# Transposing the tail rows of each routed tile on TensorE in place of VectorE

## The reference

```python
x = x + xattn(_layernorm(x), ctx_512, Wq, Wkv_expand, Wout)
x = x + bitlinear_ffn(_layernorm(x), ...)
x = x + moe(_layernorm(x), rms_weight, router_w, w_gate, w_up, w_down, sw_gate, sw_up, sw_down)

# moe, per token t with h = rmsnorm(x):
probs = softmax(h @ router_w); topv, topi = top_k(probs, 2); topv /= sum(topv)
g, u  = einsum('td,edf->tef', h, w_gate), einsum('td,edf->tef', h, w_up)
eo    = einsum('tef,efd->ted', silu(g) * u, w_down)
moe   = einsum('te,ted->td', w_dense, eo)          # 8 experts of 1024 x 512, 2 per token
out   = moe + silu(h @ sw_gate) * (h @ sw_up) @ sw_down
```

## Time and profile before

| | us |
|---|---|
| median of three runs | 651.04 (650.00 to 651.28) |
| profiled execution, its own time | 651.04 |
| its span | 648.9 |

### The profile page before, as it was taken

How to read it: one execution, slowest core, us unless ns; L and a number is a source line. 1 busy time by engine, 2 the same in 40 slices (tenths; PEclk the granted TensorE clock), 3 DMA queues, 4 the chain that set the end, 5 groups by cost and what they waited for, 6 DMA issues and landing times.

```text
span 648.9 us, 10501 instructions
## 1 busy us (share of the span) xinstructions
PE 614.7 (95%) x3604; PEld 477.7 (74%) x3605; DVE 527.8 (81%) x897; ACT 424.2 (65%) x559; POOL 147.7 (23%) x146
## 2 busy tenths in 40 slices
PE   5889999998999999969999997999999999999996
PEld 4678888886887444434557886988989889898875
DVE  5778888888587779989899558697897978979687
ACT  3988888779655969976465355376493663946530
POOL 3263446425000333427900220000000000000041
PEclk9999999999999999989999997999999999999999
DMA  8967776765236998835999556775967859678347
GB/s 329 398 271 300 299 299 234 299 259 194 98 134 253 419 384 319 331 130 201 417 377 381 194 221 232 279 310 211 375 233 277 328 209 361 227 282 342 129 152 277
DMA packets 31068, 177.87 MB, mean 274 GB/s; under 512 B 4064, under 2 KB 4064, under 8 KB 14784
## 3 DMA queue, kind: packets, MB, share of 16 engines
q1 hardware_dynamic: 25536, 158.64, 63.5%
q0 software_dynamic: 5504, 18.88, 7.7%
HBM read 154.30 MB, written 23.20 MB: 274 GB/s over the span
## 4 chain that ended last, share of the span: by engine, by line
PE 39%; DVE 23%; ACT 17%; issue 14%; DMA 3%; DVEq 2%; SPq 1%; ACTq 0%
PE BK L305 9%; PE BK L2025 9%; DVE WL L1005 7%; ACT PR L1364 5%; PE BK L2028 3%; PE BK L1771 3%; PE BK L1872 3%; ACT WH L1549 2%; PE BK L311 2%; ACT RA L1337 2%; PE BK L317 2%; PE BK L312 2%; DMA RA<-wbit 2%; DMA RX<-wqk 2%; DVE BH L887 1%
## 5 line engine op out<-in xcount | busy, mean ns | idle before, releaser
L2025 PE MATMUL BK<-EX,WH 128*128 128x320 f32 x512 | 136.2, 348 | 3.6 <-DVE EX L1030 3.2
L2028 PE MATMUL BK<-EX,WL 128*128 128x160 f32 x448 | 106.8, 238 | 0.0
L2025 PEld LDWEIGHTS BK<-EX,WH 128*128 128x128 f32 x512 | 94.2, 192 | 6.1 <-issue 3.5
L1005 DVE TENSOR_TENSOR WL<-RA,WH 128x2048 fp32r<-128x2048 f32 x40 | 89.3, 2288 | 9.6 <-ACT WH L1549 9.4
L2028 PEld LDWEIGHTS BK<-EX,WL 128*128 128x128 f32 x448 | 87.0, 194 | 0.3
L1549 ACT ACTIVATE WH<-RA 128x2048 fp32r<-128x2048 f32 x40 | 73.7, 1912 | 2.4 <-PE BK L1872 2.3
L682 POOL DMA_INDIRECT GA<-rows,SLOT x4 | 4.9, 1231 | 246.6 <-DVE WL L1005 245.7
L650 POOL TENSOR_TENSOR HB<-HB,ND (+2 forms) x28 | 31.2, 1129 | 104.8 <-DVE BH L887 104.1
L1434 ACT ACTIVATE RA<-RA,RT 128x2048 int16<-128x2048 f32 x22 | 44.2, 2020 | 9.8 <-DMA RA<-wbit 6.6
L1005 DVE TENSOR_TENSOR WL<-RC,WH 128x2048 fp32r<-128x2048 f32 x20 | 45.0, 2287 | 0.6 <-ACT WH L1549 0.6
L1826 PE MATMUL BK<-TG,XQ 128*128 128x512 bf16 x192 | 42.4, 379 | 0.1
(11 more groups left out here) (306 smaller groups left out, 1571.5 us busy)
## 6 DMA issues: line engine op xcount, KB each, us to landing
RA<-wbit SPq DMA_DIRECT2D x54, 1024.0 KB, 6.4
RA<-wmoe SPq DMA_DIRECT2D x40, 1024.0 KB, 6.5
RC<-wmoe SPq DMA_DIRECT2D x20, 1024.0 KB, 7.6
rows<-ZERO POOLq DMA_DIRECT2D x40, 256.0 KB, 12.7
XG<-rows SPq DMA_DIRECT2D x10, 512.0 KB, 3.6
rows<-YS SPq DMA_DIRECT2D x9, 512.0 KB, 6.1
RA<-wqk SPq DMA_DIRECT2D x7, 640.0 KB, 7.8
RA<-wo SPq DMA_DIRECT2D x4, 1024.0 KB, 7.3
```

Source lines behind the costliest of these rows:

```text
L1005: e.tensor_tensor(WL[m][:, q * RAW:q * RAW + RAW], RC[j][:, :], WH[m][:, q * RAW:q * RAW + RAW].bitcast(f32), ALU.subtract)\
L2025: mm = e.matmul(bank[GBK[f]][:, 0:2 * R], WH[m][:, at], EX[:, k, :, :].rearrange("p a b -> p (a b)"), start=k == 0, stop=k == KD - 1)
L2028: e.matmul(bank[GBK[f]][:, 0:R], WL[m][:, at], EX[:, k, 0, :], start=False, stop=False)
```

## The change

The tail rows are no longer transposed on VectorE. TensorE transposes them, 32 rows and 128 columns at a time, each right behind the full block of the same columns and into the same bank, so that a bank holds up to three blocks of 160 columns. That needs three banks per tile (`TB` = 0, 1, 3) in place of two, with three, three and two blocks (`TK`). The buffer `XT` goes. ScalarE and VectorE read whole blocks of 160 columns from the banks, three instructions each. The third group waits for the product that frees bank 3. In the opening of the routed part VectorE's order changes, and the third tail load of SP loses a wait.

```diff
-TB = (0, 1)
-TB_FIRST = (4, 5)
+TK = ((0, 1, 2), (3, 4, 5), (6, 7))
+TB = (0, 1, 3)
+TB_FIRST = (4, 5, 3)
...
             e.wait_ge(s("et_pe"), 2 * NS + 2)
             e.dma_start(XG[:, :], rows_dram[2 * R:2 * R + P, :]).then_inc(s("e_in"), 16)
-            e.wait_ge(s("et_lo"), 3 * NS + 1)
             e.dma_start(XY[XTAIL, :], rows_dram[2 * R + P:3 * R, :]).then_inc(s("e_in"), 16)
...
-            def tail_rows(t):
-                waits(e, ("e_in", t * 32 + 32))
-                for j in range(4):
-                    at = slice(TAIL_R * j, TAIL_R * j + TAIL_R)
-                    ins = e.transpose(XT[at, :, :], r3(XY[XTAIL, :], KD)[:, :, at])
-                ins.then_inc(s("et_lo"), 1)
             def routed_lo(t, at=TB):
-                for q in range(2):
...
+                for n, ks in enumerate(TK):
+                    e.wait_ge(s("et_hi"), t * 3 + n + 1)
+                    ins = e.tensor_tensor(EX[:, ks[0]:ks[-1] + 1, 1, :], r3(bank[at[n]][:, 0:R * len(ks)], len(ks)),
+                                          EX[:, ks[0]:ks[-1] + 1, 0, :].bitcast(f32), ALU.subtract)
+                    if n != 1:
                         ins.then_inc(s("et_lo"), 1)
...
             split(1, 0, (0,))
             e.wait_ge(s("rows"), 1)
+            hidden(NS - 1, HTKH, HTKL)
+            routed_lo(NS, TB_FIRST)
             split(1, 0, (1,))
-            hidden_product(NS - 1)
-            e.wait_ge(s("eh"), 2 * NS)
-            tail_rows(NS)
-            routed_lo(NS, TB_FIRST)
-            hidden_lo(NS - 1, HTKH, HTKL)
             split(1, 1)
...
                 gate_sum(t, 1)
-                tail_rows(t + 1)
                 routed_product(t)
...
             def routed_hi(t, at=TB):
-                for q in range(2):
-                    e.wait_ge(s("et_pe"), t * 2 + q + 1)
-                    e.activation(EX[:, 4 * q:4 * q + 4, 0, 0:P], r3(bank[at[q]], 4), ACT.Copy).then_inc(s("et_hi"), 1)
-                e.wait_ge(s("et_lo"), t * 3 + 1)
-                e.activation(EX[:, :, 0, P:R], XT[:, :, :], ACT.Copy).then_inc(s("et_hi"), 1)
+                for n, ks in enumerate(TK):
+                    if n < 2:
+                        e.wait_ge(s("et_pe"), t * 2 + n + 1)
+                    e.activation(EX[:, ks[0]:ks[-1] + 1, 0, :], r3(bank[at[n]][:, 0:R * len(ks)], len(ks)), ACT.Copy)\
+                        .then_inc(s("et_hi"), 1)
...
-            def routed_rows(t, at=TB):
-                waits(e, ("e_in", t * 32 + 32))
-                for q in range(2):
-                    rows_t(q, XG, at)
+            def routed_rows(t, ns, at=TB):
+                for n in ns:
+                    if n == 0:
+                        waits(e, ("e_in", t * 32 + 32))
+                    for i, k in enumerate(TK[n]):
+                        cs = slice(k * P, k * P + P)
+                        e.transpose(bank[at[n]][:, i * R:i * R + P], XG[:, cs], IDF[:, :])
+                        m = e.transpose(bank[at[n]][:, i * R + P:i * R + R], XY[XTAIL, cs], IDF[XTAIL, XTAIL])
+                    if n != 1:
+                        m.then_inc(s("et_pe"), 1)
...
-                    routed_rows(NS, TB_FIRST)
+                    e.wait_ge(s("ys_d"), NS)
+                    routed_rows(NS, (0, 1, 2), TB_FIRST)
...
                 waits(e, ("hsum", t * 5 + 3))
-                routed_rows(t + 1)
+                routed_rows(t + 1, (0, 1))
+                waits(e, ("hsum", t * 5 + 4))
+                routed_rows(t + 1, (2,))
```

More of the change, by code:

```diff
@@ L219, in program @@
         SI = c("SI", [P, FE], f32)
-        XT = nc.alloc_sbuf_tensor_at("XT", [P, KD, TAIL_R], f32, offset=HTH.manual_sbuf_range[0] + 4 * KE * 2 * R)
         assert c.at == HB.manual_sbuf_range[0]
@@ L1012, in rows_lo @@
                     e.tensor_tensor(EX[:, 4 * q:4 * q + 4, 1, 0:P], r3(bank[4 + q], 4),
-                                    EX[:, 4 * q:4 * q + 4, 0, 0:P].bitcast(f32), ALU.subtract).then_inc(s("et_lo"), 1 + q)
-            def tail_rows(t):
-                waits(e, ("e_in", t * 32 + 32))
-                for j in range(4):
-                    at = slice(TAIL_R * j, TAIL_R * j + TAIL_R)
-                    ins = e.transpose(XT[at, :, :], r3(XY[XTAIL, :], KD)[:, :, at])
-                ins.then_inc(s("et_lo"), 1)
-            def routed_lo(t, at=TB):
-                for q in range(2):
[L1024 to L1027, removed]
+                                    EX[:, 4 * q:4 * q + 4, 0, 0:P].bitcast(f32), ALU.subtract).then_inc(s("et_lo"), 1)
+            def routed_lo(t, at=TB):
+                for n, ks in enumerate(TK):
[3 more added lines that the diff above has]
+                    if n != 1:
                         ins.then_inc(s("et_lo"), 1)
-                e.wait_ge(s("et_hi"), t * 3 + 3)
-                e.tensor_tensor(EX[:, :, 1, P:R], XT[:, :, :], EX[:, :, 0, P:R].bitcast(f32), ALU.subtract)\
-                    .then_inc(s("et_lo"), 1)
             def gate_sum(t, q):
@@ L1606, in result @@
             def result(t):
-                waits(e, ("y2_pe", t + 1), ("y_st", t * 32 + 32), ("et_lo", t * 3 + 3))
+                waits(e, ("y2_pe", t + 1), ("y_st", t * 32 + 32), ("et_lo", t * 2 + 2))
                 e.activation(YS[:, 0:512], bank[AB[0]], ACT.Copy)
@@ L1651, in _ @@
             e.wait_ge(s("ys_d"), NS)
-            e.wait_ge(s("ht_lo"), 2 * NS)
             e.wait_ge(s("cnt"), 1)
@@ L1944, in ranks, with rows_t @@
                 m.then_inc(s("pos_pe"), 1)
-            def rows_t(q, rows, at=(4, 5)):
+            def rows_t(q, rows):
                 for k in range(4):
                     cs = slice((4 * q + k) * P, (4 * q + k + 1) * P)
-                    m = e.transpose(bank[at[q]][:, k * P:k * P + P], rows[:, cs], IDF[:, :])
+                    m = e.transpose(bank[4 + q][:, k * P:k * P + P], rows[:, cs], IDF[:, :])
                 m.then_inc(s("et_pe"), 1)
-            def routed_rows(t, at=TB):
-                waits(e, ("e_in", t * 32 + 32))
-                for q in range(2):
-                    rows_t(q, XG, at)
+            def routed_rows(t, ns, at=TB):
[8 more added lines that the diff above has]
+                        m.then_inc(s("et_pe"), 1)
             def routing(step):
@@ L1974, in tile @@
                 if not more:
-                    waits(e, ("et_lo", t * 3 + 3))
+                    waits(e, ("et_lo", t * 2 + 2))
                 for m in range(2):
@@ L1983, in tile @@
                             routing((m, q))
-                    e.wait_ge(s("et_lo"), t * 3 + 3)
+                    e.wait_ge(s("et_lo"), t * 2 + 2)
                     lows(e, bank[m], [(EX[:, k, 1, 0:P], WH[m][:, k * FE:k * FE + FE]) for k in range(KD)])\
```

## The result

| | before | after |
|---|---|---|
| median, us | 650.95 | 684.38 |
| range of the runs | 650.00 to 651.28 | 683.93 to 686.18 |
| profiled execution, its own time | 651.04 | 685.42 |
| its span | 648.9 | 683.6 |

The changed kernel is slower by 5.2% (ratio 1.0521, 95% interval 1.0499 to 1.0544). The forecast was slower by 0.6%, 654.6 us: the right sign, and a tenth of the size. The measured time lies far outside the forecast's range of 651.8 to 658.6 us.

A forecast was written before the change was run, and what follows sets the result against it. The loop was taken as bound by a 26.83 us chain through TensorE, VectorE and ScalarE, with TensorE 0.29 us from binding. Loop 1.8, end 0.55 and opening 1.2 gave 3.55 on 651.04: 654.6 us, range 651.8 to 658.6.

The forecast's parts named there:

- VectorE's saving is worth nothing in the loop: Routed loop: VectorE's 1.77 us of XT transposes are off the chain, paid back as longer wait; 0 us gain.
- 0.29 us of cover on TensorE: Routed loop: TensorE's gate-sum wait hides 0.29 us per period; the remaining 0.26 us over seven periods gives +1.8 us.
- What is added on TensorE: Each routed tile: eight small transposes at 0.069 us, spacing taken from L1933, 0.55 us per tile.
- each switch costs extra: Rival, routed tiles: each switch between 32 and 128 rows costs extra, 1.28 us per tile; 660.4 us, chance 0.05.
- my high end: TensorE's added work per tile: 1.28 us if each small transpose alternating with a full one cost 0.16 us.
- Opening: Opening of the routed part: TensorE waits for WL0's second half, starts 1.6 us later; less clock saving, +1.2 us.
- the 0.4 us that I took off: Opening: assumed saving from less work run at half clock, 0.4 us between 0.7 or 0.6 and nothing.
- End: Last routed tile: no next gate sum to hide behind, so the whole added 0.55 us counts; +0.55 us.
- the wait on hsum 5t+4: Routed loop: new wait costs nothing, as that product is issued before TensorE finishes its last part and twelve transposes.
- ScalarE's EX copies in the loop: Three copies keep 1280 columns in all, cost 0; the second, waiting for all sixteen transposes, causes no wait.
- SP's wait: Opening: dropping SP's wait on et_lo lets one load leave about 2 us earlier; worth 0.
- Signs set beforehand: Forecast wrong if period stays 26.8 or exceeds 27.4 us, or TensorE starts the first tile no later than before.

The follow-up runs named there:

- experiment 2: Changed kernel with all eight full transposes of a tile first and all eight small ones behind them; 655.83 us, ratio 1.0079 to the kernel before.
- experiment 7: Changed kernel with the opening's old order restored on VectorE (second WL0 half ahead of the EX low parts); 679.41 us, ratio 1.045 to the kernel before.
- experiment 4: Kernel before, with the eight full transposes of each routed tile issued four times over, 32 in a row; 666.67 us, ratio 1.0257.

## Why the prediction was right in sign and wrong in size

- **VectorE's saving is worth nothing in the loop: right.** All 1.77 us of it, and more, came back as its longer wait before L1032 (0.36 to about 3.1).
- **0.29 us of cover on TensorE, the rest lengthens the period: right** as a mechanism. With the small ones last (experiment 2) the period grew by 0.50 us for 0.78 us of added work, so 0.28 was covered.
- **The step that failed: "What is added on TensorE", 0.069 us per small transpose, 0.55 us per tile.** That is the cost within a run of equals, and L1933 was such a run. The changed kernel alternates. Each change of height adds 0.13 us, sixteen a tile are 2.1 us, and with 8 x 0.062 for the small ones themselves the added work is 2.6 us, nearly five times the forecast. My rival "each switch costs extra" named the mechanism and priced it at half, 1.28 us a tile from a single gap of 0.16 us, with a chance of 0.05; even its 660.4 us is 24 too low. An upper bound was in the rows: a lone transpose lasts 0.27 us against a spacing of 0.110, so a change that lets nothing overlap costs up to 0.16 by this estimate. Sixteen of them on top of the 0.55 are 3.1 us a tile, above the 2.6 measured, where my high end was 1.28. The Trainium skill says in TensorEngine Tiling (Array Packing), Key Properties, that changing the tiling mode drains TensorE. If the small transposes run in another mode than the full ones, which no view shows, the traces agree: a cost at every change of height, 0.13 us each.
- **The clock in the loop: not in the forecast at all.** This is the second step that failed, a term put at nothing: I looked for idle stretches only, and there is none. 12.6 of the 33 us, 1.6 us in each of eight tiles, come from half clock behind an unbroken run of full and small transposes in turn. No rival had it.
- **Opening: mechanism right, size short.** TensorE waited for the second half of WL0, as worked out. It started 2.8 us later and not 1.6, because the sixteen transposes ended at 394.1 and not 392.7, and everything behind them moved with that. The half clock lasted 10.2 us and not 6.8, so there was no saving to subtract: the 0.4 us that I took off had the wrong sign, and about 0.3 came on top. 3.1 in place of 1.2.
- **End: mechanism right.** The whole of a tile's added work counts there: 4.2 us, which is 2.6 and 1.6.
- **Edits costed at nothing held**: the wait on hsum 5t+4, ScalarE's EX copies in the loop, SP's wait. ScalarE did come to wait for transposes, which the sum had excluded (L1575, 11.5 us over eight tiles), but off the path: TensorE never waited for it in the loop.
- **Signs set beforehand.** I had called the forecast wrong if the period came out above 27.4 us. It is 30.7.

With the order of experiment 2 the forecast of 654.6 would have been within 1.3 us (655.83), so it came closer to a kernel that issues the small transposes together. Even there a period grew by 0.50 us and not 0.26, since two changes of height, 0.26 us, had no place in the sum.

## What to carry to other kernels

Before an instruction is priced from its spacing in a run of equals, look at what stands before and behind it in the new order: on TensorE each change between 128-row and 32-row transposes cost 0.13 us here, so issue small tiles together or give them the full height. An engine that is 95% busy is a bad place to move work to, however cheap it looks there, when the engine that loses it was waiting anyway; the same transposes moved in time, into an idle gap of their own engine, gave the only gain. And the granted clock is to be watched behind stretches of small matmuls, not only behind idle ones.

## What the runs showed of the hardware that I had not expected

- Sixteen transposes of full height (0.110 us each, 1.66 us to the next stage) are as quick as eight full and eight small ones in two runs (1.58), and twice as quick as the two kinds alternating (3.41).
- TensorE's clock fell from 1.00 to 0.50 while the engine had no idle time: behind 3.4 us of alternating transposes in 8 tiles of 8 in the changed kernel and in 5 of 8 in experiment 7's profile, 2.5 to 3.4 us into the run of small ones in 5 tiles of 8, and never behind 3.4 us of full ones. The Trainium skill, TensorE: Matmul & The Clock Gate, Part 4, says that the full clock doesn't engage for transpose mode, which doesn't count as busy in the same way. For full ones the rows of experiment 4 disagree, 1.00 throughout, and the measurement decides. Why the same run of transposes is followed by a fall in one tile and not in the next, the runs don't show. Changing the rows without the moving columns wasn't tried, so which of the two makes the change of shape cost is open.
- In the changed kernel the falls came in all eight tiles, at equal distances of 30.72 us; in the kernel of experiment 7 it began only at the fourth period and then stayed.
